# Moving the last third of the query and key projections behind the last Newton products, and the copy of the queries behind the squares of the input

## The chip, the cores and the metric

The kernel runs on one core of a Trainium2 chip. The metric is the device time of one execution in microseconds (us); lower is better. TensorE does the matrix products, VectorE (DVE), ScalarE (ACT) and GpSimd (POOL) the work on elements, SyncE (SP) issues the transfers. Each engine runs its own queue in order, and the engines wait for each other through semaphores.

## The reference

32 images of 128x128 pixels become 2048 tokens of width 192. A tokenizer with layer norm, an attention with 12 heads of which the 64x64 softmax matrix is inverted by a Newton iteration, and a mixture of 16 experts follow one another. Cut to what matters here:

```
h = _L0_tok_ref(x, gamma, beta, W, b)                # layer norm over 3840, then 3840 -> 192
qkv = (x @ w_qkv.T).reshape(B, N, 3, H, hd).transpose(2, 0, 3, 1, 4)
kernel_2 = softmax(queries_landmarks @ keys_landmarks^T)      # 64x64 per image and head
K = mat; V = 1.0 / denom * swapaxes(K, -1, -2)
for _ in range(6):
    KV = K @ V
    V = (0.25 * V) @ (13.0 * I - KV @ (15.0 * I - KV @ (7.0 * I - KV)))
out = (kernel_1 @ V) @ (kernel_3 @ v)
h = h + out @ w_proj.T + b_proj
h = h + ffn(layernorm(h))                            # 16 experts, 8 per token
```

With 64 tokens and 64 landmarks in an image, the three softmax matrices are the same one.

## The kernel before

The 2048 tokens are 16 tiles of 128 (two images each). After a setup of some 48 us comes the tile loop, `iteration(t)` for t = 0 to 15, on every engine in the same written order, and then the experts. The order is written out by hand: one iteration does the six Newton steps of tile t, and between their halves the earlier and later stages of the neighbouring tiles stand in "windows". In each step k TensorE does the squares of lanes 0 and 1 (`newton(k, 0, t, lane)`, 12 matmuls of 64x64 for each lane; the profile records each of them twice, so 48 stand for both lanes), then `first_window(k, t)`, then the products of both lanes (`newton(k, 1, t, lane)`), then `second_window(k, t)`. All Newton matmuls are issued in line 398. For the first step they read `r0` (shown as `ps<-r`), else `rr`; the products read `uu` and `qq`.

Between the halves ScalarE copies the squares from PSUM to `qq` (lines 635 to 641), VectorE forms the sum `uu` (`newton_sum`, line 844), and ScalarE copies the products to `rr` (line 644). In the last step VectorE makes `rf` of the products instead (`newton_last`, line 851, one operation for each lane). The first squares of the next tile use the same PSUM banks, so they wait for `r_ready`, which line 851 gives.

Around the seam between tile t and t + 1 stand: `transpose_xl(t + 2)` (lines 299, 300) and on ScalarE `copy_xl(t + 2)` (592) in step 4; in the first window of step 5 `qk(t + 2)`, the projections of queries and keys of tile t + 2, six matmuls of 128x128 in three column blocks w = 0, 1, 2 (lines 305 and 306, each shown as two records) into bank D. Its last one gives `qk_done`. ScalarE waits for that in `copy_q(t + 2)` (line 596), which copies columns 0 to 255 of D to `qt`, behind the copies of `y` (line 625, `save_y`). Then it does the squares of the input for the layer norm, `squares(t + 3)` (line 588, 1024 columns), which wait for the input's transfer and the mean. VectorE waits for `q_copied` in `masked_keys(t + 2)` (lines 783 and 787), which stands behind line 851 and ahead of the first sum of the next tile, and reads D too, columns 256 to 383 among it. The next step 0 has `value(t + 2)` in its first window (lines 319, 322) and `scores(t + 2)` (line 339) in its second, then VectorE's row maxima and differences (798, 800). There t counts the old tile.

SyncE loads tile t + 2's input once `squares(t)` is done (line 177).

Of the kernel before, what the change touches and what calls it, by code (L numbers as in the profile page):

```python
# [33 lines left out]
def on(f):  # L34

    return 0 <= f < NT
# [13 lines left out]
def vit_block_kernel(nc, x, xt, ws, wh, gb, tok_b, wqk, wv, wp, bp, rw, w1, w2, const, copies, out):  # L50
    with ExitStack() as ctx:
# [85 lines left out]
        def sems(names):  # L137
            return [sem(n) for n in names.split()]
# [11 lines left out]
        xltr_done, xlt_ready, qk_done, q_copied = sems("xltr_done xlt_ready qk_done q_copied")  # L150
# [127 lines left out]
        def _(pe):  # L278
# [20 lines left out]
                pe.transpose(D[:, 0:P], xl[:, 0:DA], ident)  # L299
                pe.transpose(D[:, P:2 * P], xl[:, DB:DIM], ident).then_inc(xltr_done, 1)  # L300

            def qk(t):
                pe.wait_ge(xlt_ready, t + 1)
                for w in range(3):
                    pe.matmul(D[:, w * P:w * P + P], wqk_a[:, w * P:w * P + P], xlt[:, 0, :], start=True, stop=False)  # L305
                    last = pe.matmul(D[:, w * P:w * P + P], wqk_b[:, w * P:w * P + P], xlt[:, 1, :], start=False, stop=True)  # L306
                last.then_inc(qk_done, 1)

            def value(t):
                if t >= 3:  # L310
# [91 lines left out]
            def out_heads(t):  # L402
                pe.wait_ge(r_ready, 12 * t + 12)
                pe.wait_ge(y_copied, 4 * t + 4)
                pe.wait_ge(sdiff, 2 * min(t + 3, NT) - 1)
                for i in range(2):
                    for p in range(PAIRS):
                        g, j = divmod(p, 4)
                        last = pe.matmul(D[32 * j:32 * j + 32, g * P + 64 * i:g * P + 64 * i + 64], y_t[:, t % 2, i, p, :],
                                         rf[:, p // LP, i, p % LP, :], start=True, stop=True, tile_position=(0, 32 * j))  # L410
                last.then_inc(o_done, 1)
# [20 lines left out]
            def first_window(k, t):  # L432
                if k == 0 and on(t + 1) and t >= 1:
                    value(t + 1)
                if k == 1 and on(t - 1):
                    out_heads(t - 1)
                if k == 1 and on(t + 3):
                    tok(t + 3, 0, 2)
                if k == 2 and on(t + 1):
                    transpose_kernel(t + 1)  # L440
                if k == 2 and on(t + 3):
                    tok(t + 3, 2, 4)
                if k == 3 and on(t + 1):
                    transpose_sums(t + 1)
                    gram(t + 1)
                if k == 4 and on(t + 1):
                    spread_denominators(t + 1)
                if k == 4 and on(t - 1):
                    logits(t - 1)
                if k == 5 and on(t + 2):  # L450
                    qk(t + 2)

            def second_window(k, t):
                if k == 0 and on(t + 1):
                    scores(t + 1)
                if k == 1 and on(t - 1):
                    project(t - 1)
                if k == 2 and on(t + 3):
                    tok(t + 3, 4, CH)
                if k == 3 and on(t - 1):  # L460
                    transpose_x2(t - 1)
                if k == 4 and on(t + 2):
                    transpose_xl(t + 2)
# [120 lines left out]
        def _(act):  # L584
            def squares(t):
                act.wait_ge(mu_ready, t + 1)
                act.wait_ge(x_loaded[t % 2], 16 * (t // 2 + 1))
                act.activation(sq[:], xin[t % 2], ACT.Square, bias=st[:, 0:1]).then_inc(sq_ready, 1)
# [5 lines left out]
            def copy_q(t):  # L594
                act.wait_ge(qk_done, t + 1)
                act.activation(qt[:], D[:, 0:2 * P].rearrange("p (a n) -> p a n", a=2), ACT.Copy).then_inc(q_copied, 1)
# [72 lines left out]
            def first_window(k, t):  # L669
                if k == 0 and on(t + 1) and t >= 1:  # L670
                    copy_value(t + 1)
                if k == 1 and on(t + 1):
                    exponents(t + 1)
                if k == 1 and on(t - 1):
                    copy_out(t - 1)
                if k == 5 and on(t - 1):
                    router_exp(t - 1)
                if k == 5 and on(t + 1):
                    save_y(t + 1)
                if k == 5 and on(t + 2):  # L680
                    copy_q(t + 2)

            def second_window(k, t):
                if k == 0 and t == 0:
                    squares(2)
                if k == 2 and on(t + 1):
                    copy_kernel(t + 1)
                if k in (0, 1, 2) and t == NT - 1:
                    if k == 0:
                        act.wait_ge(ffw_loaded, 64)  # L690
                    high_part(k)
                if k == 3 and on(t - 1):
                    copy_x2(t - 1)
                if k == 4 and on(t + 2):
                    copy_xl(t + 2)
                if k == 5 and on(t + 3):
                    squares(t + 3)

            def iteration(t):
                for k in range(STEPS):  # L700
# [422 lines left out]
```

## Time and profile before

| | us |
|---|---|
| median of 3 runs | 698.87 |
| lowest and highest run | 697.99, 701.11 |
| the profiled execution, its own time | 700.34 |
| its span, first to last instruction | 698.5 |

The profile is of one execution on the one core. A row of a stretch gives its bounds and length, then the busy time (and in brackets the instructions) of TensorE's matmuls, its weight loads, VectorE, ScalarE and GpSimd, the granted TensorE clock as a share of full speed, the transfers' share and their GB/s. A row of the timeline gives the start, the length from the first start to the last end, the engine and line, the operation with output <- input, and the count; in brackets the idle time before it and what ended that. PE is TensorE's matmul side, PEld its weight loads. Matmuls overlap, so a group of many lasts less than their number times the length of one. Of a whole tile the tile loop takes 24 to 27 us; the tile loop ends at about 456 us and the experts take the rest.

### The profile page before, as it was taken

The page shows a single profiled execution, that of the slowest core. Times are in us where ns is not written, and L with a number is a line of the kernel's source. Part 1 is how long each engine was busy: PE and PEld are TensorE (multiplying, and loading weights), DVE is VectorE, ACT ScalarE, POOL GpSimd, SP SyncE. Part 2 cuts the span into 40 slices and gives each one's busy share as a digit, 9 for nine tenths or more (in the row PEclk, how much of TensorE's full clock was granted, in tenths as well). Part 3 has the DMA queues.
Part 4 walks back from the last instruction along what each step waited for, and adds up shares of the span by engine and source line. Part 5 has one row for each costly group of instructions (what it writes and reads, how often), then busy time and mean ns, then how long its engine had stood idle before and what let it go on. Part 6 is the DMA issues. An engine that isn't in the chain of part 4 may idle for free.

```text
span 698.5 us, 29941 instructions
## 1 busy us (share of the span) xinstructions
PE 648.6 (93%) x13218; PEld 570.8 (82%) x13218; DVE 494.8 (71%) x1351; ACT 384.6 (55%) x1045; POOL 105.7 (15%) x328
## 2 busy tenths in 40 slices
PE   4678999999999989999999898899999999999997
PEld 2567888888888878888888787688999999999996
DVE  5557878878888888888888877576557457556743
ACT  0236666676766666676676666755333344444332
POOL 1302123113223212212212301110000000000000
PEclk9889999999999999999999999999999999999999
DMA  8793111121121121121100000000000000000000
GB/s 309 264 252 106 34 65 34 34 64 34 34 64 35 34 63 34 34 64 35 34 4 4 5 4 4 5 2 0 1 23 1 1 0 23 2 1 23 1 1 23
DMA packets 13409, 30.64 MB, mean 44 GB/s; under 512 B 1248, under 2 KB 7520, under 8 KB 13024
## 3 DMA queue, kind: packets, MB, share of 16 engines
q1 hardware_dynamic: 13280, 28.73, 12.9%
q8 instruction: 104, 1.70, 1.0%
q14 instruction: 25, 0.20, 0.1%
HBM read 27.16 MB, written 1.57 MB: 41 GB/s over the span
## 4 chain that ended last, share of the span: by engine, by line
PE 84%; DVE 6%; ACT 3%; issue 2%; DVEq 0%; ACTq 0%
PE ps L398 28%; PE ps L562 18%; PE ps L552 16%; PE ps L289 5%; PE ps L305 2%; PE ps L365 2%; PE ps L416 2%; PE ps L347 2%; PE ps L306 2%; PE ps L339 1%; DVE uu L844 1%; DVE rf L851 1%; PE ps L429 1%; DVE se L800 1%; DVE sst L798 1%
## 5 line engine op out<-in xcount | busy, mean ns | idle before, releaser
L903 DVE SCALAR_TENSOR_TENSOR acc<-ps,comb,acc 128x192 f32<-128x192 f32 x256 | 89.1, 410 | 83.9 <-PE ps L562 83.8
L562 PE MATMUL ps<-w_sb,work 128*128 128x192 f32 x768 | 140.4, 326 | 0.7 <-ACT work L731 0.7
L562 PEld LDWEIGHTS ps<-w_sb,work 128*128 128x128 f32 x768 | 129.5, 189 | 9.5 <-issue 1.1
L731 ACT ACTIVATE work<-ps 128x512 f32<-128x512 f32 x96 | 57.3, 597 | 137.8 <-PE ps L552 137.8
L398 PEld LDWEIGHTS ps<-rr 64*64 64x64 f32 x3840 | 98.2, 135 | 22.9 <-issue 14.7
L398 PE MATMUL ps<-rr 64*64 64x64 f32 x3840 | 110.9, 223 | 6.4 <-issue 5.3
L844 DVE SCALAR_TENSOR_TENSOR uu<-rr,qq 128x384 f32<-128x384 f32 x160 | 86.5, 563 | 32.9 <-ACT qq L637 25.8
L398 PE MATMUL ps<-uu,qq 64*64 64x64 f32 x4608 | 96.0, 224 | 11.0 <-DVE uu L844 10.2
L644 ACT ACTIVATE rr<-ps 128x384 f32<-128x384 f32 x160 | 73.4, 489 | 56.3 <-PE ps L398 55.9
L398 PEld LDWEIGHTS ps<-uu,qq 64*64 64x64 f32 x4608 | 80.8, 134 | 26.4 <-DVE uu L844 16.1
L641 ACT ACTIVATE qq<-ps 128x384 f32<-128x384 f32 x96 | 47.1, 491 | 8.8 <-PE ps L398 3.0
L289 PE MATMUL ps<-weff,xtb 128*128 128x193 f32 x240 | 50.7, 348 | 1.3 <-DVE t L755 1.1
L552 PE MATMUL ps<-xhi,wah 128*128 128x512 f32 x96 | 50.4, 525 | 0.0
L289 PEld LDWEIGHTS ps<-weff,xtb 128*128 128x128 f32 x240 | 40.0, 197 | 4.0 <-DMA xtb<-xt_dram 1.7
L637 ACT ACTIVATE qq<-ps 64x192 f32<-64x192 f32 x128 | 41.6, 325 | 3.1
L635 ACT ACTIVATE qq<-ps 128x192 f32<-128x192 f32 x64 | 21.2, 331 | 37.2 <-PE ps L398 35.7
L552 PE MATMUL ps<-xhi,wb 128*128 128x512 f32 x96 | 38.1, 397 | 0.0
L552 PE MATMUL ps<-xlo,wb 128*128 128x512 f32 x96 | 38.0, 396 | 0.0
L552 PE MATMUL ps<-xhi,wal 128*128 128x512 f32 x96 | 37.7, 393 | 0.0
L552 PE MATMUL ps<-xlo,wah 128*128 128x512 f32 x96 | 37.2, 387 | 0.0
L895 DVE TENSOR_TENSOR wal<-w_a,wah 128x128 fp32r<-128x128 f32 x96 | 27.3, 285 | 8.7 <-ACT wb L667 8.7
L398 PE MATMUL ps<-r 64*64 64x64 f32 x768 | 25.8, 219 | 7.5 <-DVE rf L851 7.5
(142 smaller groups left out, 1066.7 us busy)
## 6 DMA issues: line engine op xcount, KB each, us to landing
xtb<-xt_dram SPq DMA_DIRECT2D x16, 512.0 KB, 3.5
work<-x_dram SPq DMA_DIRECT2D x16, 512.0 KB, 3.7
wsh<-ws_dram SPq DMA_DIRECT2D x10, 288.0 KB, 5.5
w_sb<-w_dram SPq DMA_DIRECT2D x1, 2304.0 KB, 23.4
w_a<-w_dram SPq DMA_DIRECT2D x1, 1536.0 KB, 11.5
w_b<-w_dram SPq DMA_DIRECT2D x2, 768.0 KB, 15.9
out_dram<-acc SPq DMA_DIRECT2D x4, 384.0 KB, 2.6
mult<-copies_dram SPq DMA_DIRECT2D x1, 512.0 KB, 8.3
```

The source lines that it names most:

```text
L289: last = pe.matmul(C[:, 0:DIM + 1], xtb[:, t % 2, c, :], weff[:, c, :], start=(c == 0), stop=(c == CH - 1))
L398: last = pe.matmul(ps[z:z + 64, 2 * lane + i, 64 * j:64 * j + 64], lhs[r, lane, i, j, :], rhs[r, lane, i, j, :], start=True, stop=True)
L552: last = pe.matmul(ps[:, UPB[n % 3], :], w[:, k, :], xs[:, half, tok4], start=(m == 0), stop=(m == 4))
L562: last = pe.matmul(ps[:, 2 + 2 * (e % 2) + j // 2, (j % 2) * DIM:(j % 2 + 1) * DIM], hid[:, n % 4, j * P:(j + 1) * P], w2_sb[:, c, :], sta ...
L635: act.activation(q[:, 0], ps[:, 0, 0:LC], ACT.Copy).then_inc(q_ready, 1)
L637: act.activation(q[a:a + 64, 1], ps[64 - a:128 - a, 1, 0:LC], ACT.Copy).then_inc(q_ready, 1)
L641: act.activation(q, ps[:, 2:4, 0:LC], ACT.Copy).then_inc(q_ready, 1)
L644: act.activation(rr[:, lane].rearrange("p i h n -> p i (h n)"), ps[:, 2 * lane:2 * lane + 2, 0:LC], ACT.Copy, scale=0.25).then_inc(r_ready, 1)
L731: act.activation(hid[:, n % 4, :], ps[:, UPB[n % 3], :], ACT.Gelu_apprx_tanh).then_inc(gelu_done, 1)
L844: dve.scalar_tensor_tensor(out=uu[:, lane], in0=src[:, lane], scalar=3.0, in1=qq[:, lane], op0=ALU.mult, op1=ALU.add).then_inc(u_ready, 1)
L895: dve.tensor_tensor(w[r, k, :], raw[r, col:col + P], high[r, k, :].bitcast(F32), ALU.subtract).then_inc(wlo_ready, 1)
L903: last = dve.scalar_tensor_tensor(out=a, in0=ps[:, 2 + 2 * (e % 2) + j // 2, (j % 2) * DIM:(j % 2 + 1) * DIM], scalar=comb[:, g * GT + j, ...
```

## The change

`qk` gets a range of column blocks. In the first window of step 5 only blocks 0 and 1 are projected; block 2 follows in the second window, behind the last products. `qk_done` is given by block 2's last matmul as before, so it comes later. On ScalarE `copy_q(t + 2)` moves from the first window of step 5 to the second, behind `squares(t + 3)`. In the setup `qk(0)` and `qk(1)` keep all three blocks in one, and the order of the copy and the squares there is as it was. VectorE's order is unchanged.

```diff
-            def qk(t):
-                pe.wait_ge(xlt_ready, t + 1)
-                for w in range(3):
+            def qk(t, w0=0, w1=3):
+                if w0 == 0:
+                    pe.wait_ge(xlt_ready, t + 1)
+                for w in range(w0, w1):
                     pe.matmul(D[:, w * P:w * P + P], wqk_a[:, w * P:w * P + P], xlt[:, 0, :], start=True, stop=False)
                     last = pe.matmul(D[:, w * P:w * P + P], wqk_b[:, w * P:w * P + P], xlt[:, 1, :], start=False, stop=True)
-                last.then_inc(qk_done, 1)
+                if w1 == 3:
+                    last.then_inc(qk_done, 1)
...
                 if k == 5 and on(t + 2):
-                    qk(t + 2)
+                    qk(t + 2, 0, 2)
 
             def second_window(k, t):
+                if k == 5 and on(t + 2):
+                    qk(t + 2, 2, 3)
...
                 if k == 5 and on(t + 1):
                     save_y(t + 1)
-                if k == 5 and on(t + 2):
-                    copy_q(t + 2)
...
                 if k == 5 and on(t + 3):
                     squares(t + 3)
+                if k == 5 and on(t + 2):
+                    copy_q(t + 2)
```

TensorE at a seam, from the last squares of step 5 to the first squares of the next tile; a row with "waits" is the first matmul of a lane. Before:

```order
L398 MATMUL ps<-rr 64x64 x11
L305 MATMUL ps<-xlt,wqk_a 128x128 [waits xlt_ready]
L306 MATMUL ps<-xlt,wqk_b 128x128
L305 MATMUL ps<-xlt,wqk_a 128x128
L306 MATMUL ps<-xlt,wqk_b 128x128
L305 MATMUL ps<-xlt,wqk_a 128x128
L306 MATMUL ps<-xlt,wqk_b 128x128
L398 MATMUL ps<-uu,qq 64x64 [waits u_ready]
L398 MATMUL ps<-uu,qq 64x64 x11
L398 MATMUL ps<-uu,qq 64x64 [waits u_ready]
L398 MATMUL ps<-uu,qq 64x64 x11
L398 MATMUL ps<-r 64x64 [waits r_ready,r0_ready]
```

The same place in the changed kernel, where the lines have shifted by one or two:

```order
L400 MATMUL ps<-rr 64x64 x11
L306 MATMUL ps<-xlt,wqk_a 128x128 [waits xlt_ready]
L307 MATMUL ps<-xlt,wqk_b 128x128
L306 MATMUL ps<-xlt,wqk_a 128x128
L307 MATMUL ps<-xlt,wqk_b 128x128
L400 MATMUL ps<-uu,qq 64x64 [waits u_ready]
L400 MATMUL ps<-uu,qq 64x64 x11
L400 MATMUL ps<-uu,qq 64x64 [waits u_ready]
L400 MATMUL ps<-uu,qq 64x64 x11
L306 MATMUL ps<-xlt,wqk_a 128x128
L307 MATMUL ps<-xlt,wqk_b 128x128
L400 MATMUL ps<-r 64x64 [waits r_ready,r0_ready]
```

One pair of projection matmuls has moved from ahead of the products to behind them, ahead of the next tile's squares.

ScalarE at the same seam, from the copy of lane 1's last squares (qq) to the first copies of the next tile; y_t is `save_y`, qt the copy of the queries, sq the squares of the input. Before:

```order
L641 ACTIVATE qq<-ps 128x384 [waits square_done]
L625 ACTIVATE y_t<-ps 64x6x16 [waits m0_scaled]
L625 ACTIVATE y_t<-ps 64x6x16 x3
L596 ACTIVATE qt<-ps 128x256 [waits qk_done]
L588 ACTIVATE sq<-work,st 128x1024 [waits x_odd_loaded,mu_ready]
L639 ACTIVATE qq<-ps 128x384 [waits square_done]
```

In the changed kernel, its lines shifted by four:

```order
L645 ACTIVATE qq<-ps 128x384 [waits square_done]
L629 ACTIVATE y_t<-ps 64x6x16 [waits m0_scaled]
L629 ACTIVATE y_t<-ps 64x6x16 x3
L592 ACTIVATE sq<-work,st 128x1024 [waits x_odd_loaded,mu_ready]
L600 ACTIVATE qt<-ps 128x256 [waits qk_done]
L643 ACTIVATE qq<-ps 128x384 [waits square_done]
```

The squares and the copy have traded places.

## Rows read from the trace of the kernel before

**Rows 1.** The page, the chain that ended last, shares by engine.

```profile
PE 84%; DVE 6%; ACT 3%; issue 2%; DVEq 0%; ACTq 0%
```

**Rows 2.** Stretches from one tile's first squares to the next's: busy time by engine.

```profile
204.45:229.75 25.30, 24.60 (x744) 21.53 (x744) 21.31 (x55) 17.75 (x48) 6.52 (x20) 1.00 0.15 45
255.21:282.23 27.02, 24.85 (x744) 21.64 (x744) 21.48 (x55) 17.51 (x48) 6.23 (x20) 1.00 0.14 43
```

**Rows 3.** Waits of TensorE, 75 to 410 us: us in total, times, longest.

```profile
PE ps L398 <- DVE rf L851: 7.2, 14, 0.8
PE ps L398 <- issue: 4.9, 8, 1.3
```

**Rows 4.** Timeline of TensorE at the seam of tiles 6 and 7, 225.0 to 229.9.

```profile
225.59 1.26 PE L398 MATMUL ps<-rr 64*64 64x64 f32 x48
226.79 0.49 PE L305 MATMUL ps<-xlt,wqk_a 128*128 128x128 f32 x2
227.12 0.39 PE L306 MATMUL ps<-xlt,wqk_b 128*128 128x128 f32 x2
227.34 0.39 PE L305 MATMUL ps<-xlt,wqk_a 128*128 128x128 f32 x2
...
228.01 0.39 PE L306 MATMUL ps<-xlt,wqk_b 128*128 128x128 f32 x2
228.32 0.93 PE L398 MATMUL ps<-uu,qq 64*64 64x64 f32 x48
229.75 0.35 PE L398 MATMUL ps<-r 64*64 64x64 f32 x5 [0.49 <-DVE rf L851]
```

**Rows 5.** Timeline of VectorE there; the last row is of the narrower stretch 227.9 to 229.0.

```profile
227.30 1.07 DVE L844 SCALAR_TENSOR_TENSOR uu<-rr,qq 128x384 f32<-128x384 f32 x2 [0.35 <-ACT qq L637]
229.04 1.02 DVE L851 SCALAR_TENSOR_TENSOR rf<-ps,cst 128x384 f32<-128x384 f32 x2 [0.67 <-PE ps L398]
229.98 0.41 DVE L783 TENSOR_TENSOR kb_a<-ps,cst 128x256 f32<-128x256 f32 x1
230.43 0.42 DVE L787 TENSOR_TENSOR kb_b<-ps,cst 64x256 f32<-64x256 f32 x1
231.28 1.20 DVE L844 SCALAR_TENSOR_TENSOR uu<-r,qq 128x384 f32<-128x384 f32 x2 [0.43 <-ACT qq L639]
...
227.82 0.56 DVE L844 SCALAR_TENSOR_TENSOR uu<-rr,qq 128x384 f32<-128x384 f32 x1
```

**Rows 6.** The chain there, start and length; "issue" is unexplained waiting.

```profile
229.04 0.57 DVE rf L851
229.61 0.14 issue
```

**Rows 7.** Step 0 of the next tile: TensorE, the second sum, one product's length (min/median/max ns).

```profile
232.10 1.01 PE L398 MATMUL ps<-uu,qq 64*64 64x64 f32 x48
...
231.92 0.56 DVE L844 SCALAR_TENSOR_TENSOR uu<-r,qq 128x384 f32<-128x384 f32 x1
...
L398 PE MATMUL ps<-uu,qq x48: 218/218/267, 228.3 to 229.0; 64*64 64x64 f32 x48
```

**Rows 8.** The chain in step 1, between a sum's end and its products' start.

```profile
236.62 0.04 issue
```

**Rows 9.** The seam of tiles 14 and 15, which has no projections: VectorE and TensorE.

```profile
431.45 1.07 DVE L844 SCALAR_TENSOR_TENSOR uu<-rr,qq 128x384 f32<-128x384 f32 x2 [0.29 <-ACT qq L637]
...
432.06 1.09 PE L398 MATMUL ps<-uu,qq 64*64 64x64 f32 x48 [1.02 <-DVE uu L844]
```

**Rows 10.** Timeline of ScalarE at the seam of tiles 6 and 7.

```profile
228.65 0.36 ACT L596 ACTIVATE qt<-ps 128x256 f32<-128x256 f32 x1
228.91 1.14 ACT L588 ACTIVATE sq<-work,st 128x1024 f32<-128x1024 f32 x1
230.76 0.49 ACT L639 ACTIVATE qq<-ps 128x384 f32<-128x384 f32 x1 [0.71 <-PE ps L398]
```

**Rows 11.** The page, transfers of the input: KB each, us to landing.

```profile
work<-x_dram SPq DMA_DIRECT2D x16, 512.0 KB, 3.7
```

## The prediction

> **What bounds the kernel now.** The page comes first: in the chain that ended last TensorE has 84% of the span, VectorE 6% and ScalarE 3% [rows 1]. The change touches only the tile loop, so the next view is the table of stretches from the first matmul of one tile's Newton iteration to that of the next: 25.30 us for a normal tile, of which TensorE's matmuls fill 24.60 at a granted clock of 1.00, and 27.02 for a bad one with nearly the same busy time (24.85) [rows 2]. So a tile costs what TensorE has queued, plus its pauses. The waits from 75 to 410 us name the pauses [rows 3]: 7.2 us in 14 pieces behind the line 851 operation (the last Newton sum on VectorE) and 4.9 us in 8 that the profile can't name ("issue"). The 14 pieces lie at the seam between two tiles, exactly where the change works.
>
> The timeline of one seam shows why [rows 4, 5]. Everything here is from that seam (tile 6 to 7). The sequence is: squares of step 5, six groups of projection matmuls (L305, L306; two records each), 48 last products, then a pause of 0.49 us, then the first squares of the next tile (`ps<-r`, 229.75). The pause is the time of line 851 for lane 0: it starts at 229.04, its share of the chain is 0.57, then 0.14 until the squares start [rows 6]. Each of the 14 calls of qk inside the loop (t = 0 to 13) has such a seam.
>
> **The projection matmuls that move.** Per seam two of six instructions move from before the products to behind them. Four L305/L306 groups in a row start 0.22 us apart [rows 4], so a third of the projections, two groups, takes 0.45 us, and the products' first instruction could issue that much earlier: at 228.32 - 0.45 = 227.87. It then waits for the first sum of lane 0. VectorE does both sums in 227.30 + 1.07, the second alone is 227.82 + 0.56 = 228.38 [rows 5]; so the first ends about 227.86, and with the 0.04 that the chain shows between a sum and its products [rows 8] lane 0's products start at 227.90: 0.42 earlier. Lane 1's can't keep that: they need the sum that ends at 228.38. How soon the last product starts after that sum is seen twice where the sum does bind. In step 0 the second sum ends at 231.92 + 0.56 = 232.48, the 48 products end at 232.10 + 1.01 = 233.11, and one lasts 0.22 [rows 7], so the last starts at 232.89, 0.41 after the sum. At the seam that has no projections (tile 14 to 15) it is 431.45 + 1.07 = 432.52 and 432.06 + 1.09 - 0.22 = 432.93, again 0.41 [rows 9]. So at a changed seam the last product starts at 228.38 + 0.41 = 228.79, instead of 228.32 + 0.93 - 0.22 = 229.03: 0.24 earlier, not 0.45.
>
> Behind it stands the moved block, and it is dearer there than where it was. It must be entered from the 64x64 tiles and left to them again, a second time per seam. The row prices both: the last square starts at 225.59 + 1.26 - 0.22 = 226.63 and the first L305 at 226.79, 0.15 later (the 48 squares start 0.02 apart, 226.63 - 225.59 over 47); the first L305 group takes 0.33 to the next group's start (instead of 0.22); the last L306 group takes 0.31 to the first product's start (228.01 to 228.32) [rows 4]. The moved block therefore takes 0.15 + 0.33 + 0.31 = 0.79 us from the last product to the first square of the next tile. The work on TensorE grows by 0.79 - 0.45 = 0.34 a seam; the 0.49 of pause pays for it.
>
> Squares of the next tile: 228.79 + 0.79 = 229.58. The other thing that they wait for, line 851 of lane 0, starts 0.72 after the first product (228.32 to 229.04), so at 227.90 + 0.72 = 228.62, and lets them go at 228.62 + 0.57 + 0.14 = 229.33 [rows 6]. It is no longer last. **Gain per seam: 229.75 - 229.58 = 0.17 us.** The bounds: if the entry and exit cost nothing there, the squares go at 229.33 and the gain is 0.42; if the last products don't move at all, the squares go at 229.03 + 0.79 = 229.82, a loss of 0.07. I take 0.17, because both of its terms are measured at the same kinds of instruction, the entry and exit at the very seam.
>
> The Trainium skill, "TensorEngine Tiling (Array Packing)", section Key Properties, says that changing the tiling mode, as against the tile within a mode, drains TensorE, which speaks against this change. The trace agrees: 0.15 and the longer groups appear exactly at the change between 64x64 and 128x128. Without that rule the sum would be the 0.42 above, with it 0.17.
>
> **The copy of the queries.** On ScalarE the copy and the squares of the input trade places. Before: the copy of the queries behind the copies of y (line 625), at 228.65 for 0.36, the squares from 228.91 for 1.14, then idle until 230.76 [rows 10]. After: the squares take 228.65 to 229.79. Their inputs are no wait: the transfer of the input is issued once the squares two tiles earlier have freed the buffer, some 50 us before, and lands in 3.7 us [rows 11]. The moved block's last matmul starts at 228.79 + 0.15 + 0.33 + 0.11 = 229.38 (0.11 being half a group's spacing) and lasts 0.28 (0.39 less 0.11), so `qk_done` comes at 229.66, within the squares. The copy starts at 229.69 to 229.79 (neighbours on ScalarE overlap by up to 0.10) and ends at 230.05 to 230.15. ScalarE's next task, line 639, moves to 230.76 - 0.17 = 230.59, so nothing is late on ScalarE.
>
> The new wait is on VectorE: the masked keys (lines 783, 787) wait for that copy, with the first sum of the next tile queued behind them and, behind that sum, TensorE's products of step 0. They started at 229.98; now at about 230.10 to 230.20. The second starts 0.45 after the first and lasts 0.42 [rows 5], so both are done at 230.97 to 231.07. The sum wants to start at 231.28 - 0.17 = 231.11. It fits, by 0.04 to 0.14. Even a little more is covered: in step 0 the products wait for the second sum, which starts at 231.92 behind ScalarE's copy, while VectorE could have taken it 0.52 after the first (the distance in step 5, 227.30 to 227.82), 0.12 earlier. The scores, which need the copy and the keys, stand behind the products of step 0, after 233.1 [rows 7].
>
> **The sum.** 14 seams x 0.17 = 2.4 us. Against the profiled execution, span 698.5 and time 700.34, that is 696.1 and 697.9; against the median of the runs, 698.87, it is **696.5 us**. The rest of the iteration and the expert stage only shift: what VectorE does in step 1 hangs on the scores, which hang on TensorE. A measurement of this kernel tells about 0.5%, 3.5 us, from no change; the forecast is below that.
>
> **The rivals.** *Free refill*: TensorE enters and leaves the block while it would have waited anyway, and the squares start when line 851 allows, at 229.33. For it: 0.49 us of pause and 0.45 of work fit each other. Against it: entry and exit are paid in queue order, and all are seen in rows where no semaphore holds TensorE. 14 x 0.42 = 5.9 us, 693.0.
>
> *The last products stay*: lane 1's products gain nothing, because lane 0's and their own sum overlap differently. Then 14 x 0.07 = 1.0 us more, 699.9. Against it: 0.41 after the sum at two places.
>
> *The masked keys become the wait* (slower). Place: VectorE between line 851 and the first sum of the next tile. It decides from the moment that the second masked key ends after about 231.23 (231.11 plus the 0.12 of cover), so if the copy ends 0.16 to 0.26 later than worked out. Every further tenth goes straight to the products of step 0, the scores and the row maxima. For a seam to come out 0.30 us worse than before, the keys must end at 231.70 (231.23 + 0.17 + 0.30), 0.63 to 0.73 later than worked out: the squares would have to start that much later than line 625 lets them, or the copy to wait for an engine that this trace doesn't show. 14 x 0.30 = 4.2 us, 703.1. Against it: the squares and the copy have no other input, and their lengths are on record [rows 10].
>
> *Lost in the pauses*: the stretches differ by up to 1.7 us with the same busy time [rows 2], by pauses with no named cause. If these absorb or shift with the gain, nothing is left: 698.9, give or take 1.5.
>
> **How the numbers follow.** Forecast 0.60; free refill 0.12; last products stay 0.14; masked keys 0.06; lost in the pauses 0.08. Faster by over 0.5% needs 0.25 us a seam: the free refill, and a small part of the forecast's spread, 0.17. Slower by over 0.5%: the masked keys and a tail, 0.07. Within: 0.76. The range goes from 693.0, the free refill, to 700.5, which takes in the products that stay and the pauses; the slower rival is left out.
>
> **What would show it.** In the profile after: the two moved groups between the last `ps<-uu,qq` and the first `ps<-r`, last product to first square 0.79 instead of 0.71; second sum to last product 0.41 instead of 0.65; no waits of TensorE on line 851 at the changed seams; the sequence squares, copy on ScalarE with the copy starting near 229.7 in this seam's time; and the first sum of the next tile behind a copy (line 639) and not behind the second masked key. The prediction is wrong if the first squares follow line 851 by 0.14 (gain 0.42), if the first sum follows the masked keys directly and late, or if the seams win 2.4 us and the stretches between them give it back.

## The result and the profile after

The changed kernel takes 696.08 us (median of 14 runs, 693.84 to 699.38), the kernel before 701.07 (14 runs beside it, 697.99 to 702.36). The ratio is 0.9935, with a 95% interval of 0.9918 to 0.9952: 0.65% faster, 4.6 us with an interval of 3.4 to 5.7. The forecast time, 696.5, lies 0.4 us from the measured one, but that flatters it: 14 runs put the kernel before at 701.07, not at the 698.87 of the first three. The difference was forecast as 2.4 us and measured as 4.6. So there are two questions: are the 2.4 us where the prediction put them, and what of the other 2, of which the interval leaves 1.0 to 3.3.

The seams first. TensorE at the same seam as [rows 4], here in the changed kernel (its lines are one or two higher; start, length, engine, line, operation, count):

```profile
227.28 0.49 PE L306 MATMUL ps<-xlt,wqk_a 128*128 128x128 f32 x2
227.60 0.39 PE L307 MATMUL ps<-xlt,wqk_b 128*128 128x128 f32 x2
227.83 0.39 PE L306 MATMUL ps<-xlt,wqk_a 128*128 128x128 f32 x2
228.05 0.39 PE L307 MATMUL ps<-xlt,wqk_b 128*128 128x128 f32 x2
228.41 1.09 PE L400 MATMUL ps<-uu,qq 64*64 64x64 f32 x48
229.43 0.49 PE L306 MATMUL ps<-xlt,wqk_a 128*128 128x128 f32 x2
229.75 0.39 PE L307 MATMUL ps<-xlt,wqk_b 128*128 128x128 f32 x2
230.07 0.33 PE L400 MATMUL ps<-r 64*64 64x64 f32 x4
```

The last product starts at 228.41 + 1.09 - 0.22 = 229.28, the first squares of the next tile at 230.07: 0.79, to the hundredth what entry, first group and exit were priced at, and there is no wait left ahead of the squares. VectorE there, to be held beside [rows 5]:

```profile
227.79 1.07 DVE L848 SCALAR_TENSOR_TENSOR uu<-rr,qq 128x384 f32<-128x384 f32 x2 [0.35 <-ACT qq L641]
229.12 1.07 DVE L855 SCALAR_TENSOR_TENSOR rf<-ps,cst 128x384 f32<-128x384 f32 x2 [0.26 <-PE ps L400]
230.59 0.42 DVE L787 TENSOR_TENSOR kb_a<-ps,cst 128x256 f32<-128x256 f32 x1 [0.40 <-ACT qt L600]
231.05 0.43 DVE L791 TENSOR_TENSOR kb_b<-ps,cst 64x256 f32<-64x256 f32 x1
231.62 1.20 DVE L848 SCALAR_TENSOR_TENSOR uu<-r,qq 128x384 f32<-128x384 f32 x2
```

The second sum ends at 228.86, 0.42 ahead of the last product. The masked keys now wait 0.40 for the copy of the queries (L600) and end at 231.48; the next sum starts 0.14 later and has no wait of its own recorded. ScalarE, beside [rows 10]:

```profile
228.32 0.91 ACT L629 ACTIVATE y_t<-ps 64x96 f32<-64x96 f32 x4
229.14 1.14 ACT L592 ACTIVATE sq<-work,st 128x1024 f32<-128x1024 f32 x1
230.18 0.38 ACT L600 ACTIVATE qt<-ps 128x256 f32<-128x256 f32 x1
```

The copy starts 0.10 before the squares end. TensorE's waits from 75 to 406 us, beside [rows 3] (us in total, times, longest):

```profile
PE ps L400 <- issue: 3.1, 6, 1.0
PE ps L400 <- DVE uu L848: 2.0, 6, 1.0
PE ps L411 <- issue: 1.0, 2, 0.7
PE ps L359 <- DVE csum L817: 0.3, 1, 0.3
```

The 14 waits for the last Newton sum, 7.2 us, are gone. (At one seam, into tile 13, the sum still is the last to come: the squares start 0.15 after its end there, but the view lists no wait.) In the chain TensorE has risen from 84% [rows 1] to:

```profile
PE 86%; DVE 5%; ACT 3%; issue 1%; DVEq 0%
```

And the stretches from one tile's first squares to the next's, beside [rows 2]: a tile without pause, and one with.

```profile
255.21:280.35 25.14, 25.05 (x744) 21.74 (x744) 21.46 (x55) 17.60 (x48) 6.30 (x20) 1.00 0.16 46
280.35:306.32 25.97, 25.09 (x744) 21.74 (x743) 21.41 (x55) 17.69 (x48) 6.12 (x20) 1.00 0.14 44
```

25.14 against 25.30, so 0.16 to 0.17 a tile. Read seam by seam, from the end of the second sum to the next squares, the change saves 0.09 us at the first of the 14 seams, about 0.16 at twelve and 0.40 at the one into tile 13: 2.4 us in all, so the first question is answered. The second is that of the pauses that the profile calls issue.

### The profile page after: what moved, and what is told of

Read it like the earlier page. It is cut to its first block, busy times and chain, and to the rows that moved or that the text cites. A ratio compares the mean times of both kernels' runs of the same rounds, so it can differ in the third digit from the quotient of the medians.

```text
span 696.3 us, 29941 instructions
## 1 busy us (share of the span) xinstructions
PE 654.2 (94%) x13218; PEld 571.8 (82%) x13218; DVE 495.9 (71%) x1351; ACT 385.6 (55%) x1045; POOL 105.1 (15%) x328
## 4 chain that ended last, share of the span: by engine, by line
PE 86%; DVE 5%; ACT 3%; issue 1%; DVEq 0%
PE ps L400 29%; PE ps L566 18%; PE ps L556 16%; PE ps L289 5%; PE ps L306 2%; PE ps L367 2%; PE ps L418 2%; PE ps L349 2%; PE ps L307 2%; DVE uu L848 1%; PE ps L341 1%; DVE se L804 1%; DVE sst L802 1%; PE ps L431 1%; PE ps L321 1%
## 5 line engine op out<-in xcount | busy, mean ns | idle before, releaser
L400 PE MATMUL ps<-uu,qq 64*64 64x64 f32 x4608 | 98.4, 225 | 11.1 <-DVE uu L848 10.7
L289 PE MATMUL ps<-weff,xtb 128*128 128x193 f32 x240 | 49.0, 339 | 1.3 <-DVE t L759 1.1
L289 PEld LDWEIGHTS ps<-weff,xtb 128*128 128x128 f32 x240 | 38.2, 190 | 4.0 <-issue 2.0
L899 DVE TENSOR_TENSOR wb<-w_b,wb 64x128 fp32r<-64x128 f32 x96 | 27.8, 290 | 3.0
```

What stands on the lines that cost most here:

```text
L289: last = pe.matmul(C[:, 0:DIM + 1], xtb[:, t % 2, c, :], weff[:, c, :], start=(c == 0), stop=(c == CH - 1))
L400: last = pe.matmul(ps[z:z + 64, 2 * lane + i, 64 * j:64 * j + 64], lhs[r, lane, i, j, :], rhs[r, lane, i, j, :], start=True, stop=True)
L899: dve.tensor_tensor(w[r, k, :], raw[r, col:col + P], high[r, k, :].bitcast(F32), ALU.subtract).then_inc(wlo_ready, 1)
```

## The experiments

Theory A: the seams give 2.4 us and the rest comes out of the pauses, which are TensorE's instructions arriving late when a tile's input transfer is under way. Theory B: the swap on ScalarE has a gain of its own. All times below are medians, the ratio is to the kernel before run beside it, with its 95% interval. Those runs of the kernel before had a median of 701.07 us in the first round (the changed kernel), 700.82 in the second (to noload_after in the table), 700.94 in the third (to no_block2) and 700.01 in the last, so kernels of different rounds are compared by their ratios.

In all kernels the tile without pause and the sum of the pauses are read the same way: starts of the first `ps<-r` matmul of tiles 1 to 12 and their distances; the shortest distance is the tile without pause, what the 11 distances have above it is the sum of the pauses (of the one profiled execution).

| kernel | time | ratio | tile without pause | pauses in 11 tiles |
|---|---|---|---|---|
| before | 701.07 | 1 | 25.30 | 5.9 |
| changed | 696.08 | 0.9935 (0.9918 to 0.9952) | 25.14 | 4.4 |
| swap_only | 701.47 | 1.0010 (0.9994 to 1.0025) | 25.31 | 7.5 |
| split_only | 698.11 | 0.9965 (0.9951 to 0.9980) | 25.38 | 2.6 |
| noload_before | 695.10 | 0.9923 (0.9903 to 0.9943) | 25.29 | 0.2 |
| noload_after | 691.72 | 0.9877 (0.9856 to 0.9899) | 25.14 | 0.4 |
| before_late | 698.32 | 0.9963 (0.9945 to 0.9980) | 25.30 | 3.7 |
| after_late | 696.95 | 0.9939 (0.9915 to 0.9962) | 25.15 | 4.5 |
| after_late2 | 696.59 | 0.9932 (0.9911 to 0.9954) | 25.14 | 4.0 |
| no_block2 | 695.42 | 0.9931 (0.9906 to 0.9956) | 24.89 | 5.9 |
| two_behind | 701.46 | 1.0016 (1.0003 to 1.0029) | 25.58 | 4.3 |
| copy_late2 | 697.93 | 0.9975 (0.9961 to 0.9989) | 25.39 | 1.8 |
| after_halves | 693.32 | 0.9909 (0.9887 to 0.9931) | 25.13 | 2.3 |
| after_quarters | 693.13 | 0.9897 (0.9875 to 0.9919) | 25.13 | 0.3 |

### Each half of the change alone

swap_only, against the kernel before:

```diff
-                if k == 5 and on(t + 2):
-                    copy_q(t + 2)
...
                 if k == 5 and on(t + 3):
                     squares(t + 3)
+                if k == 5 and on(t + 2):
+                    copy_q(t + 2)
```

> Only ScalarE's half of the change: the copy of the queries behind the squares of the input, with all six projection matmuls still ahead of the last products. Theory A (the seams give 14 x 0.17 = 2.4 us through TensorE alone, the rest of the 4.6 us comes out of pauses of TensorE that the profile calls issue, whose places in its queue are fixed and whose length is set by what the transfers do at that moment): the seams stay as before, second sum to first squares 1.37 us, and the time is within 1 to 2 us of before, less only if the pauses are shorter, since the squares end 0.26 us earlier and so release the next input transfer earlier. Theory B (the surplus of 2.2 us is the swap's own, by earlier squares on ScalarE): 2.2 us faster, with a shorter tile even in tiles without a pause. The masked keys wait until about 230.2 of the seam's time, later than the last sums, and should cost nothing, as the next sum starts at 231.28.

It is 0.7 us slower than before, with no change in the interval, and its tile without pause is the old one:

```profile
202.72:228.03 25.31, 24.62 (x743) 21.52 (x744) 21.42 (x55) 17.77 (x49) 6.55 (x20) 1.00 0.14 45
228.03:254.84 26.81, 24.87 (x743) 21.60 (x744) 21.42 (x55) 17.76 (x49) 6.55 (x20) 1.00 0.13 43
```

Theory B is out. The pauses didn't get shorter with the earlier transfer either; in this execution they are the longest of all.

split_only, against the changed kernel:

```diff
+                if k == 5 and on(t + 2):
+                    copy_q(t + 2)
                 if k == 5 and on(t + 3):
                     squares(t + 3)
-                if k == 5 and on(t + 2):
-                    copy_q(t + 2)
```

> Only TensorE's half: the third block of projections behind the last products, and on ScalarE the copy of the queries still ahead of the squares, both in the second window. The seam on TensorE should look as in the changed kernel (0.41 from the second sum to the last product, 0.79 to the first squares). But the copy can start only at 229.69 in the seam's time, so the squares run 229.95 to 231.09, and ScalarE's copy of the next tile's first squares, wanted at 230.59, starts at about 231.0; lane 1's, wanted at 231.23, at about 231.4. Step 0's second sum and products are then 0.17 late and the gain of the seam is gone: within 1 us of before plus or minus the pauses. If instead the surplus is the split's own, this is as fast as the full change, 4.6 us under before.

The seam on TensorE is that of the changed kernel, and the squares do hold ScalarE up, as expected (timeline of ScalarE; the first squares of this tile start at 229.47):

```profile
229.58 0.38 ACT L600 ACTIVATE qt<-ps 128x256 f32<-128x256 f32 x1 [0.94 <-PE ps L307]
229.86 1.14 ACT L592 ACTIVATE sq<-work,st 128x1024 f32<-128x1024 f32 x1
230.90 0.48 ACT L643 ACTIVATE qq<-ps 128x384 f32<-128x384 f32 x1
231.27 0.49 ACT L645 ACTIVATE qq<-ps 128x384 f32<-128x384 f32 x1
```

```profile
204.08:229.47 25.39, 25.05 (x744) 21.67 (x744) 21.38 (x55) 17.69 (x47) 6.55 (x20) 1.00 0.15 45
```

The copy of the squares runs 1.43 after the seam instead of 1.01 (230.76 - 229.75, [rows 4, 10]). The cost was expected as 0.17 and is 0.25 (25.39 against 25.14), so this tile is 0.08 longer than the kernel's before: without the swap the split would lose 14 x 0.08 = 1.1 us. And yet the kernel is 0.35% (2.5 us) faster than before. That was not expected, and what is there to explain it is the pauses: 2.6 us against 5.9, in one profile each. What it changed beside the seam is the moment of the input's transfer, which is issued when the squares end: here 1.53 us after the seam, in the kernel before 0.30, in the changed one 0.21, in swap_only 0.05.

### The kernels without the tiles' transfers

In both kernels:

```diff
-            for t in range(4, NT):
-                tile_loads(t)
...
-                    pe.wait_ge(xt_loaded[t % 2], 16 * (t // 2 + 1))
+                    pe.wait_ge(xt_loaded[t % 2], 16 * min(t // 2 + 1, 2))
...
-                act.wait_ge(x_loaded[t % 2], 16 * (t // 2 + 1))
+                act.wait_ge(x_loaded[t % 2], 16 * min(t // 2 + 1, 2))
```

> The kernel before without the input transfers of tiles 4 to 15: the tiles read the four loads that are there, over and over, so the result is not the reference's. Theory A: the pauses called issue come from TensorE's instructions arriving late when a tile's transfer is under way, so most of the 4.9 us of them (8 waits) go, tiles come near the 25.30 us of a tile without pause, and the time falls by 3 to 5 us. Rival (the pauses have nothing to do with the transfers): the pauses stay, and the time stays within 1 us.

> The changed kernel with the same transfers left out. Theory A: its pauses go too, tiles take 25.14 us, and its distance to the kernel before without the transfers is what the seams give, 2.4 us, and not 4.6. Theory B or any other in which the surplus is in the order of the work: the distance stays at 4 to 5 us.

5.4 us and 4.1 us less than the same kernels with the transfers (0.77% and 0.9877/0.9935, 0.58%), the first give or take 1.4, the second some 2, and no wait named issue is left. Their engines do the same work as before, on old input, so the results are not the reference's. TensorE's waits from 75 to 406 us, all that the view lists, in noload_before:

```profile
PE ps L396 <- DVE rf L849: 7.2, 14, 0.8
PE ps L396 <- DVE uu L842: 2.7, 10, 1.0
PE ps L355 <- DVE csum L811: 0.3, 1, 0.3
```

and in noload_after:

```profile
PE ps L398 <- DVE uu L846: 3.1, 13, 1.0
PE ps L357 <- DVE csum L815: 0.3, 1, 0.3
```

So nearly all of the unnamed pauses need a tile's transfer; what stays is 0.2 and 0.4 us in the 11 tiles (0.29 of it in one tile of noload_after). From the first squares of tile 1 to those of tile 15, with 13 changed seams between them, the profiles give 352.23 and 350.09 us: 2.14, where the seams read one by one give 2.3 and that one tile takes 0.29 back. By the ratios the two kernels are 3.2 us apart, from six runs each, with an interval of some 2 us to either side, which holds the 2.4 but also the 4.6; the single profiles also differ by 0.9 in the expert stage (see the end). The seams' part stands.

### What a pause is

A pause of over 0.25 us is found by comparing each distance between neighbouring matmuls with the same distance in the other tiles. The longest of the kernel before, on TensorE, in the middle of the squares of step 1:

```profile
259.10 0.45 PE L398 MATMUL ps<-rr 64*64 64x64 f32 x12
260.82 1.04 PE L398 MATMUL ps<-rr 64*64 64x64 f32 x36 [1.26 <-issue]
```

The same place in the changed kernel:

```profile
259.11 1.55 PE L400 MATMUL ps<-rr 64*64 64x64 f32 x48
```

Counted in matmuls of TensorE's whole queue, with the fixed places left out where a sum always holds it, the pauses stand at these numbers:

```
before          1108 1871 2633 3015 3395 3777 6318 6699 7080 7462 8224 8605
changed         1108 1871 2633 3015 3395 4794 7080 7462 7842 8605
swap_only       1108 1871 2633 3015 3395 5555 6318 7080 7462 8224
split_only      3015 3395 6699 7462 8605
after_halves    1871 1998 3015 7080 7462 7842
after_late2     2380 3395 4157 6827 7589 8605
```

Every distance is a whole multiple of 127.2 (763 = 6 x 127.2, 382 = 3 x, 127 = 1 x), in every kernel, though different work stands at these numbers: TensorE's queue comes in blocks of 127.2 matmuls and as many weight loads, 254 instructions and a wait or two. The page of the kernel before gives q8, the DMA queue that it calls instruction, 104 transfers with 1.70 MB, 16 KB each; 16 KB over 254 instructions is 64 bytes each, and TensorE has 2 x 13218 instructions, which makes 104 such blocks. A pause is thus a block of TensorE's own instructions that comes late. Which block is late is set by the transfers: in the tile loop there are some six blocks a tile, and the pauses of the kernels before and changed end 5.0 to 6.3 us behind the seam (the input's transfer is issued at 0.2 to 0.3 and lands 3.7 later [rows 11]) or 19.0 to 19.5 us (the transposed input, issued at 13.7 to 14.8), but for the one at 4794. By the transfer records the block of the long pause started only at 258.4 in the kernel before; the data of the input's transfer started at 256.5, and 0.51 of its 0.52 MB had started before the block. In the changed kernel the block started at 256.6, with the first of the data, and there is no pause. The queues in the kernel before from 253.0 to 258.3, where q8 has no row yet, and in the changed one from 253.0 to 256.7:

```profile
q1 hardware_dynamic: 131, 0.51, 32.6%
...
q1 hardware_dynamic: 14, 0.06, 11.2%
q8 instruction: 1, 0.02, 2.9%
```

The transfer records also say when each block has arrived. At all 86 pauses of over 0.25 us in the fourteen profiles, whatever their length, TensorE goes on 1.1 to 1.6 us after the end of the last 16 KB record before it; at the block boundaries that it crosses without a pause in the kernel before, the record ended 1.3 to 4.4 us earlier. So the block that arrives is the one that TensorE waits for. In the kernel before a block's record starts mostly 0 to 1.6 us after TensorE has crossed the boundary ahead of it, so it is fetched about one block ahead; at 258.4 it starts 2.5 us after. (The one such pause in a kernel without the transfers, 0.32 us at 8605 in noload_before, made its tile no longer.)

The Trainium skill, "Runtime: NRT & Kernel Launch", section Instruction fetch mechanics, says that instructions are refilled in 16 KiB blocks of 256 by a queue of the sequencer's own, and that crossing a block is mostly hidden. The block size agrees with the 254. Nearly hidden it is here only without the tiles' transfers: with them the crossings cost 5.4 us in the kernel before.

### The moment of the transfers

before_late and after_late, in both kernels:

```diff
                 if t >= 2:
                     sp.wait_ge(sq_ready, t - 1)
+                if t >= 4:
+                    sp.wait_ge(kb_ready, 2 * t - 4)
                 sp.dma_start(xin[b], x[t]).then_inc(x_loaded[b], 16)
```

after_late2 has beside it:

```diff
                     sp.wait_ge(tok_done, t - 1)
+                if t >= 4:
+                    sp.wait_ge(t1_ready, t - 1)
```

> The kernel before, with one thing changed: the input transfer of a tile (512 KB, issued when the squares end, 0.3 us after the first squares of the next tile) also waits for the masked keys, which end some 1.1 us after them. No engine's work changes. Theory A (TensorE's unnamed pauses are instruction fetches that come behind a tile's transfer): the pauses of step 1, 138 to 166 matmuls behind the seam, get much shorter or vanish, as in split_only where the transfer was issued 1.5 us after the seam; 1 to 3 us faster than before, tiles without pause stay at 25.3. Rival (the order of TensorE's own work makes the pauses shorter in the changed kernel): no change, within 0.7 us.

> The changed kernel with the same delay of the input transfer: the masked keys end 1.4 us after the seam instead of the squares at 0.2. Theory A: the tiles without pause stay at 25.14, the pauses of step 1 go, 1 to 2.5 us faster than the changed kernel, so 0.8 to 1.0% under before. Rival: as the changed kernel, 0.65% under before.

> As after_late, and the transfer of the transposed input, issued when the tokens' matmuls end (13.8 us after the seam), also waits for the sum on VectorE that reads their result (some 16.9 us after the seam). Theory A: the second place of the pauses, 528 to 578 matmuls behind the seam, changes too. If later is better there as well, another 0.5 to 1.5 us; if the delay meets the next fetch, the pauses move or grow by as much. It tells whether later helps as such or only where it is clear of a fetch.

before_late moves nothing on any engine but one transfer by 0.8 us and is 0.37% faster (0.20% to 0.55%, 2.6 us); its pauses at 1108, 1871, 2633 and 6318 are gone, those at 3395 (1.65 us, before 0.28) and 7462 (1.12 us, before 0.33) are longer. TensorE's waits named issue in 75 to 406 us, in before_late:

```profile
PE ps L411 <- issue: 1.9, 2, 1.4
PE ps L400 <- issue: 1.2, 2, 1.0
```

Among the kernels that leave nothing out this speaks most clearly for theory A. But after_late gains nothing on the changed kernel, 0.9939 beside 0.9935: of its pauses the early ones (1108, 1871, 2633) went too, but those at 3395 (0.93 to 1.21) and 8605 (0.46 to 1.01) grew, and new ones stand at 3777, 6699 and 8224 (0.37, 0.82 and 0.40), so that the sum is the same, 4.5 beside 4.4. after_late2 moves the second kind by one block, from 6699 to 6827 and from 7462 to 7589; against after_late they are three instead of five (2.0 us instead of 2.7), which the time, 0.9932, doesn't tell from 0.9939. Later is not better as such; it chooses which block is hit. The expectation for after_late, 1 to 2.5 us, was wrong.

### The transfers in pieces

after_halves cuts each of the two transfers of a tile into two pieces by partitions, after_quarters into four, with later events ahead of the later pieces. The core of after_quarters, against the changed kernel:

```diff
-                sp.dma_start(xin[b], x[t]).then_inc(x_loaded[b], 16)
+                rows = [slice(i * P // 4, (i + 1) * P // 4) for i in range(4)]
+                for i, r in enumerate(rows if t >= 4 else [slice(0, P)]):
+                    if i == 1:
+                        sp.wait_ge(kb_ready, 2 * t - 4)
+                    if i == 2:
+                        sp.wait_ge(scores_done, t - 2)
+                    if i == 3:
+                        sp.wait_ge(sdiff, 2 * t - 4)
+                    sp.dma_start(xin[b][r], x[t][r]).then_inc(x_loaded[b], 16)
```

> The changed kernel with each tile's two input transfers (512 KB each) cut in two pieces of 64 partitions, the second piece issued later: for the input behind the scores (about 4 us after the seam), for the transposed input behind the last gram matmuls (about 16 us). The bytes and the work of the engines are the same. If a pause is an instruction fetch that has to stand behind a whole transfer, it can now stand only behind half of one: the pauses of over 1 us go, tiles without pause stay at 25.14, and the time is 1 to 3 us under the changed kernel, between it and the 691.7 us of the one without transfers. If a delay of a fetch by any transfer is enough, the pauses are as long or more frequent, and the time is the same or up to 1 us worse.

> The same with four pieces of 32 partitions each, issued at about 0.2, 1.4, 4 and 6.5 us (input) and 13.8, 16, 17 and 19.5 us (transposed input) after the seam. First theory: shorter pauses still, 2 to 4 us under the changed kernel, 692 to 694 us. Second: more collisions, as the changed kernel or worse.

0.91% and 1.03% faster than before (693.32 and 693.13 us, four runs each); against the changed kernel, by the ratios, 1.8 and 2.7 us, each give or take 2, so that only four pieces are clear of the noise there, and barely. The bytes are the same, the tiles hold 25.13 and 25.14, and nearly all pauses are gone with four pieces: a block of instructions then stands behind 128 KB at a time, not behind 512. The kernel before was not run with its transfers in pieces. Two stretches of after_quarters, and TensorE's waits from 75 to 406 us:

```profile
98.87:124.00 25.13, 24.92 (x744) 21.66 (x743) 21.43 (x55) 17.76 (x48) 6.52 (x20) 1.00 0.16 46
300.13:325.27 25.14, 25.09 (x744) 21.78 (x744) 21.45 (x55) 17.77 (x48) 6.52 (x20) 1.00 0.19 46
...
PE ps L420 <- DVE uu L868: 2.8, 11, 1.0
PE ps L431 <- issue: 0.3, 1, 0.3
```

It has the lowest median of the complete kernels. Whether four pieces are better than two the medians don't tell; the sum of the pauses does, 0.3 against 2.3 us, in one execution of each.

### The prices of the seam

no_block2 leaves out the moved block:

```diff
-                    qk(t + 2, 0, 2)
+                    qk(t + 2, 0, 2, True)
...
-                    qk(t + 2, 2, 3)
+                    pass
```

(with True the second block gives `qk_done`.)

> The changed kernel without its moved block: in the loop the third block of projections is left out, and the masked keys read old values, so the result is not the reference's. It prices the block where it now stands. By the prediction's sum the seam is then as that of tiles 14 to 15, last product to first squares 0.55 us instead of 0.79, and nothing else is shorter: 14 x 0.24 = 3.4 us faster than the changed kernel, tiles of 24.90. If the block were hidden in the wait for line 851 (the free refill), the gain would be near 0.

Its tile without pause is 24.89 us, forecast 24.90, and at its seams the last product stands 0.55 ahead of the squares:

```profile
74.83:99.73 24.90, 24.43 (x740) 21.22 (x740) 20.51 (x48) 17.51 (x48) 6.32 (x20) 1.00 0.15 46
99.73:126.51 26.78, 24.55 (x740) 21.33 (x740) 21.61 (x55) 17.69 (x48) 6.15 (x20) 1.00 0.13 43
```

The block is not hidden: 0.24 us of it stand open at each seam, as the sum had it. But by the ratios (0.9931 beside 0.9935) the kernel is only 0.3 us faster than the changed one, not 3.4, with an interval of some 2 us to either side: four matmul records less per tile shift the blocks, and the tile in the second row alone loses 1.9 us to two pauses. Its pauses come to 5.9 us, 1.5 more than the changed kernel's, in one profile each; the other half of what is missing isn't explained. A gain of 0.24 a seam can vanish from the time and stay in the tiles.

two_behind moves a second block:

```diff
-                    qk(t + 2, 0, 2)
+                    qk(t + 2, 0, 1)
...
-                    qk(t + 2, 2, 3)
+                    qk(t + 2, 1, 3)
```

> Two of the three blocks of projections behind the last products, only the first ahead of them. The first sum (VectorE) still holds the products at 227.90 of the seam's time, so nothing starts earlier than in the changed kernel; the block behind is 0.79 + 0.45 = 1.24 us from the last product to the first squares, and they go at 228.38 + 0.41 + 1.24 = 230.03 instead of 229.58: 14 x 0.45 = 6.3 us slower than the changed kernel, tiles of 25.59. The keys, 0.45 later too, keep their slack. If the time behind the products were still free, the loss would be less than 0.45 a seam.

```profile
203.95:229.53 25.58, 24.96 (x744) 21.67 (x743) 21.43 (x54) 17.87 (x47) 6.52 (x20) 1.00 0.14 45
```

25.58 against a forecast of 25.59, and 0.16% slower than before, 0.8% behind the changed kernel (5.7 us; forecast 6.3). Of none, one and two blocks behind the products, one gives the shortest tile.

copy_late2 puts two more copies ahead of the copy of the queries:

```diff
             def copy_q(t, extra=0):
                 act.wait_ge(qk_done, t + 1)
+                for m in range(extra):
...
+                    act.activation(spare[:, m], D[:, 0:2 * P], ACT.Copy).then_inc(spare_done, 1)
```

> The changed kernel with two further copies of the same shape on ScalarE ahead of the copy of the queries, into a spare tile, 0.28 us each: the copy of the queries and the masked keys come 0.55 us later. It tests the slower rival's place and deciding point. Measured in the changed kernel, the keys end 0.14 us ahead of the first sum of the next tile, and the products of step 0 hang on the second sum, with 0.12 more. So a delay of 0.55 should cost 0.55 - 0.14 - 0.12 = 0.29 us a seam, 4.1 us in all, tiles of 25.43. If there were no cover, 0.55 x 14 = 7.7 us; if the keys were not on the path, nothing.

VectorE at a seam of copy_late2 (first squares at 226.58), where the keys have become the wait:

```profile
227.65 0.42 DVE L793 TENSOR_TENSOR kb_a<-ps,cst 128x256 f32<-128x256 f32 x1 [0.95 <-ACT qt L606]
228.11 0.43 DVE L797 TENSOR_TENSOR kb_b<-ps,cst 64x256 f32<-64x256 f32 x1
228.56 1.02 DVE L854 SCALAR_TENSOR_TENSOR uu<-r,qq 128x384 f32<-128x384 f32 x2
```

```profile
201.18:226.58 25.40, 25.02 (x745) 21.67 (x744) 21.34 (x55) 18.32 (x50) 6.52 (x20) 1.00 0.14 45
```

The copy starts 0.65 after the seam instead of 0.11 (230.18 - 230.07), the sum right behind the keys, and the tile takes 25.40: 0.54 of delay cost 0.26, so 0.28 are covered, where 0.26 were worked out. The slower rival exists at its place; the changed kernel passes it by 0.28 us. The time shows less of it, 2.8 us by the ratios against 14 x 0.26 = 3.6, and this execution had few pauses, 1.8 us.

## Why the prediction was right, and where it wasn't

- *The last products move by 0.24, not 0.45* (0.41 behind the second sum): 0.42 at every changed seam. Right.
- *The moved block takes 0.79*: 0.79 at 13 of the 14 seams; at the last but one (tile 13) line 851 starts late in both kernels, by 0.35 before, and the distance is 0.90 instead of 1.06. Right, and no_block2 and two_behind price the same steps at 0.24 and 0.44.
- *Line 851 is no longer last*: its 14 waits are gone, and it is last at one seam only, into tile 13, where it starts late. *Gain per seam 0.17*: 25.30 to 25.14. The free refill (0.42) and the products that stay (-0.07) are out.
- *The masked keys fit, by 0.04 to 0.14*: by 0.14, and copy_late2 confirms the further cover.
- *14 x 0.17 = 2.4 us*: right for the seams, 2.4 read one by one. It is partly luck that the sum comes out so well: the first seam gives 0.09 and the one into tile 13 0.40, and the two make up for each other. As the size of the whole it was half of what was measured, 4.6 (3.4 to 5.7). The step that falls short is "the rest of the iteration and the expert stage only shift", and with it the rival *lost in the pauses*: it saw the pauses, took them to be chance and as something that could only eat the gain or scatter it by 1.5 us. They are worth 5.4 us in the kernel before and 4.1 in the changed one, so by these medians the change took 1.3 us out of them, and 0.9 us is left that neither seams nor pauses explain. But the 1.3 has an interval of over 2 us to either side: that the pauses have a cause and a price is shown, that they are where the surplus of 2.2 us comes from is only likely. The single profiles agree with it (5.9 and 4.4 us).
- The time outcome "within 0.5%" had 0.76, "faster by over 0.5%" 0.17, and the latter came. The time itself fell where it was forecast, which is luck in part, since the three first runs of the kernel before were low by 2.2 us.

Open: why just the changed kernel has shorter pauses than the one before. The moment of the transfer against the seam differs by only 0.09 us (0.30 and 0.21), and the pauses don't follow it in one direction: 0.05 gave more, 1.1 to 1.5 gave less in two kernels and not in after_late, and copy_late2, with 0.21 as in the changed kernel, had 1.8 us of pauses instead of 4.4. With a block of 127.2 matmuls every 4.3 us (25.14 x 127.2 / 744) against transfers of 3 to 4 us, a few tenths can decide which block is hit, as at 258.4 and 256.6 above; each kernel has one profile only, so how far executions of one kernel differ in their pauses isn't shown. That a late block is the cause is shown by the places, by the records of the blocks, by the kernels without transfers and by before_late; by what rule the chip orders the two kinds of transfer stays open.

A second thing can have its part in the surplus and was not separated: the granted clock. Of the 59 runs of the kernel before in the last three rounds, the 25 with a mean granted clock of 0.994 or more have a median of 699.7 us, the 34 below it 701.1. In the two profiles the kernel before has 0.97 in the stretch from 47 to 100 us and the changed one 1.00. Whether the runs of the first round differ in this by more than chance isn't on record for the kernel before.

## What to carry to other kernels

A wait at a seam is no free room: price the entry into another tile shape, the exit and what bounds the piece ahead of it, and fill only as much as fits. A block moved behind a wait also moves what its last instruction releases; look which engine takes that and how much cover stands behind it. And when tiles of the same work differ in length by pauses without a name, count at which instruction they stand before calling them chance: here cutting the input transfers into four spaced pieces gave 2.7 us (give or take 2) on top of the change under study, whose seams gave 2.4.

## What the runs showed of the hardware

TensorE's instructions come in blocks of 16 KB, and one of them that comes late beside a 512 KB transfer of data stopped TensorE for up to 1.65 us (before_late, at 3395); TensorE goes on 1.1 to 1.6 us after the block's record ends. Tiles without a pause agree to about 0.03 us within a kernel. What is outside them moves without relation to what was changed: the 14 profiles have 47.4 to 50.7 us ahead of the first squares, 265.0 to 265.2 or 265.9 us from tile 15's first squares to the end, and 25.5 to 27.5 us for the tile loop's first tile. There the five longest (26.1 and more) are those with a granted clock of 0.97 between 47 and 100 us; the other nine have 1.00. So 2 to 3 us between two single executions of this kernel say nothing.
